# Output projection of a Mamba2 layer with tokens on the output partitions, one matmul group moved ahead of another, and one unused state dropped

## The reference, cut to what matters

```
x = x + 0.5 * ffn(layernorm(x))
x = x + mamba2(layernorm(x))       # 64 heads of 64 channels, state size 128, conv of 4 taps
x = x + 0.5 * ffn(layernorm(x))

# the end of mamba2, per token:
hidden = (Y_diag + Y_off + D * xs) * silu(gate)          # 4096 channels
var    = mean(hidden * hidden)
hidden = hidden * rsqrt(var + EPS) * norm_w
return hidden @ out_proj_w                               # 4096 -> 256

# the state that one chunk hands to the next:
state[c + 1] = chunk_decay[c] * state[c] + states[c]
```

## Time and profile before

| | us |
|---|---|
| median of 3 runs | 1360.67 (1360.49 to 1361.19) |
| the profiled execution | 1359.91 |
| its span, first to last instruction | 1358.2 |
| TensorE busy with matmuls | 1299.9 (96%) |
| VectorE busy | 1187.0 (87%) |
| ScalarE busy | 1001.7 (74%) |
| GpSimd busy | 851.0 (63%) |

### The profile page before, as it was taken

One profiled execution on the slowest core, in us unless ns is written; L12 is line 12 of the kernel. 1 busy time (PEld: TensorE's weight loads), 2 busy tenths in 40 slices (PEclk: granted clock), 3 DMA queues, 4 the chain that ended last, 5 costly groups with the idle time before them and its releaser, 6 DMA issues.

```text
span 1358.2 us, 26981 instructions
## 1 busy us (share of the span) xinstructions
PE 1299.9 (96%) x8896; PEld 1111.2 (82%) x8896; DVE 1187.0 (87%) x2651; ACT 1001.7 (74%) x2043; POOL 851.0 (63%) x920
## 2 busy tenths in 40 slices
PE   7999998899999999999999999999999999987998
PEld 7988886678888888888888888888888888876887
DVE  6965567899999999999999999999999999997542
ACT  1135566898888888889888888888898888883432
POOL 1033220268697878778787978787787879674232
PEclk9999999999999999999999999999999999998999
DMA  7110002265555543544555555436446544345000
GB/s 163 80 69 32 17 16 70 71 137 125 108 126 116 119 119 109 115 106 110 120 124 107 123 118 123 112 110 113 106 115 120 123 115 115 100 103 202 16 17 32
DMA packets 98106, 136.51 MB, mean 101 GB/s; under 512 B 23760, under 2 KB 45872, under 8 KB 97840
## 3 DMA queue, kind: packets, MB, share of 16 engines
q1 hardware_dynamic: 97968, 134.78, 41.7%
HBM read 124.78 MB, written 9.96 MB: 99 GB/s over the span
## 4 chain that ended last, share of the span: by engine, by line
PE 56%; DVE 29%; issue 11%; ACT 3%; DMA 0%; DVEq 0%; POOL 0%; SPq 0%; ACTq 0%; POOLq 0%
PE psum L38 13%; PE psum L40 12%; PE psum L39 12%; DVE xs L1266 6%; PE psum L1715 6%; DVE inner L1317 4%; PE psum L1704 4%; PE psum L1495 4%; DVE M L1293 3%; PE psum L1692 3%; DVE xend L1283 3%; DVE psum L1325 3%; DVE mixed L1347 2%; PE psum L1681 1%; DVE carry L1317 1%
## 5 line engine op out<-in xcount | busy, mean ns | idle before, releaser
L826 ACT ACTIVATE M<-cum_row,cum_table 128x128 f32<-128x128 f32 x1024 | 312.1, 390 | 0.0
L1266 DVE SCALAR_TENSOR_TENSOR xs<-psum,conv_w_sb,xs 128x509 f32<-128x509 f32 (+2 forms) x384 | 283.1, 737 | 0.4
L986 POOL TENSOR_TENSOR hid_lo<-hid,hid_hi 128x512 fp32r<-128x512 f32 x128 | 204.9, 1601 | 56.1 <-PE psum L40 49.9
L1032 POOL TENSOR_TENSOR hid<-hid,sg 128x512 f32<-128x512 f32 x128 | 165.8, 1295 | 76.4 <-DVE hid L1334 76.2
L1018 POOL TENSOR_TENSOR squares<-squares,sq 128x512 f32<-128x512 f32 x124 | 161.1, 1299 | 71.8 <-ACT sq L803 71.8
L1293 DVE TENSOR_TENSOR M<-M,CB 128x1024 f32<-128x1024 f32 x128 | 184.4, 1440 | 0.0
L1715 PE MATMUL psum<-M,xdt 128*64 128x128 f32 x2048 | 140.1, 278 | 20.2 <-DVE psum L1325 20.0
L1715 PEld LDWEIGHTS psum<-M,xdt 128*64 128x64 f32 x2048 | 110.1, 136 | 42.8 <-DVE M L1293 24.2
L1692 PE MATMUL psum<-xend,B_tok 128*128 128x128 f32 x1024 | 137.6, 277 | 5.3 <-DVE carry L1317 4.5
L840 ACT ACTIVATE xs<-psum,conv_b_sb,conv_w_sb 128x512 f32<-128x512 f32 x128 | 99.2, 775 | 57.3 <-PE psum L40 56.6
L834 ACT ACTIVATE M<-M 128x1024 f32<-128x1024 f32 x128 | 134.5, 1051 | 0.5
(11 more groups left out here) (197 smaller groups left out, 3379.1 us busy)
## 6 DMA issues: line engine op xcount, KB each, us to landing
cum_row<-cum_scratch SPq DMA_DIRECT2D x256, 256.0 KB, 4.6
e_row<-e_scratch SPq DMA_DIRECT2D x256, 128.0 KB, 3.5
xw_raw<-L_attn_in_proj_w_dram SPq DMA_DIRECT2D x32, 128.0 KB, 5.0
wo_raw<-L_attn_out_proj_w_dram SPq DMA_DIRECT2D x32, 128.0 KB, 4.5
gw_raw<-L_attn_in_proj_w_dram SPq DMA_DIRECT2D x16, 256.0 KB, 5.5
x_res<-_attn_hidden_states_dram SPq DMA_DIRECT2D x4, 512.0 KB, 7.1
x_scratch<-x_res SPq DMA_DIRECT2D x4, 512.0 KB, 2.6
x_res<-x_scratch SPq DMA_DIRECT2D x1, 2048.0 KB, 8.5
```

The costliest lines, as they stand in the source:

```text
L826: last = nc.scalar.activation(M[:, v % 3, h, c * CH:(c + 1) * CH], cum_row[:, v % 2, h, c * CH:(c + 1) * CH], ACT.Relu, bias=scalar_of(CUM ...
L986: nc.gpsimd.tensor_tensor(hid_lo[:], hid[:, v % 2, :], hid_hi[:, v % 2, :].bitcast(F32), ALU.subtract).then_inc(hid_lo_done, 1)
L1032: nc.gpsimd.tensor_tensor(hid[:, v % 2, :], hid[:, v % 2, :], sg[:, v % 8, :], ALU.mult).then_inc(hid_done, 1)
L1266: nc.vector.scalar_tensor_tensor(xs[:, v % 7, shift:], psum[:, X_BANK + v % 2, 0:TT - shift], tap_of(v, step), xs[:, v % 7, shift:], ALU.m ...
```

## The change

Four things are done. (1) `out_proj` holds 128 tokens of the hidden values in the array and streams the 256 columns of the output weights, for each of the slot's 4 chunks: 12 matmuls of 256 columns in place of 6 of 512. `mixed` then has tokens on the partitions, and `turn_mixed` goes, with its semaphore. `second_residual` reads `mixed` from SBUF. (2) TensorE does proj_g(s+8) ahead of diag(s+1). (3) VectorE does skip_path(s+1) behind tap 2 and scan 2. (4) The last chunk's state isn't made any more: on the last tile `to_chunk_end` and `states` work on 3 chunks, not 4.

```diff
-    mixed = sb("mixed", [P, KT, L], F32)
+    mixed = sb("mixed", [P, NC, D], F32)
...
-                nc.vector.tensor_tensor(xend[:], psum[:, XT_BANK, :].rearrange("p (c h q) -> p c h q", h=2, q=HP),
-                                        per_chunk_head(TO_END, v), ALU.mult).then_inc(xend_done, 1)
+                n = min(CPT, NC - 1 - at_slot(v)[1] * CPT)
+                nc.vector.tensor_tensor(xend[:, 0:n], psum[:, XT_BANK, 0:n * P].rearrange("p (c h q) -> p c h q", h=2, q=HP),
+                                        per_chunk_head(TO_END, v)[:, 0:n], ALU.mult).then_inc(xend_done, 1)
...
                 for m in range(KT):
+                    rows = mixed[:, t * CPT + 2 * m:t * CPT + 2 * m + 2, :].rearrange("p s d -> p (s d)")
                     if v < SLOTS:
-                        nc.vector.tensor_copy(mixed[:, m, tile(t)], psum[:, OUT_BANK + m, :]).then_inc(mixed_done, 1)
+                        nc.vector.tensor_copy(rows, bank(OUT_BANK + m)).then_inc(mixed_done, 1)
                     else:
-                        nc.vector.tensor_tensor(mixed[:, m, tile(t)], psum[:, OUT_BANK + m, :], mixed[:, m, tile(t)],
-                                                ALU.add).then_inc(mixed_done, 1)
+                        nc.vector.tensor_tensor(rows, bank(OUT_BANK + m), rows, ALU.add).then_inc(mixed_done, 1)
...
-                dve.wait_ge(mixed_turned, T + 1)
+                dve.wait_ge(mixed_done, KT * (ALL // GP - NT + T + 1))
                 for s in range(T * CPT, (T + 1) * CPT):
-                    half = psum[:, mixed_banks(T)[s % CPT // 2], s % 2 * D:(s % 2 + 1) * D]
-                    nc.vector.scalar_tensor_tensor(x3[:, s, :], half, rms[:, s:s + 1], x3[:, s, :],
+                    nc.vector.scalar_tensor_tensor(x3[:, s, :], mixed[:, s, :], rms[:, s:s + 1], x3[:, s, :],
                                                    ALU.mult, ALU.add).then_inc(x2_done, 1)
...
-                if alive(s + 1):
-                    skip_path(s + 1)
                 if alive(s + 7):
                     conv_tap(s + 7, 2)
                 if alive(s + 2):
                     scan(s + 2, 2)
+                if alive(s + 1):
+                    skip_path(s + 1)
...
-                for c in range(CPT):
+                for c in range(min(CPT, NC - 1 - t * CPT)):
                     last = nc.tensor.matmul(psum[:, ST_BANK, c * P:(c + 1) * P], B_tok[:, t * CPT + c, :],
...
-                for m in range(KT):
-                    cols = slice(m * P, (m + 1) * P)
-                    last = split_matmul(nc, psum[:, OUT_BANK + m, :], wo_hi[:, j, cols], wo_lo[:, j, cols],
-                                        hid_hi[:, v % 2, :], hid_lo[:], start=(j == 0), stop=(j == GP - 1))
+                for c in range(CPT):
+                    toks = slice(c * CH, (c + 1) * CH)
+                    last = split_matmul(nc, bank(OUT_BANK + c // 2)[:, (c % 2) * D:(c % 2 + 1) * D],
+                                        hid_hi[:, v % 2, toks], hid_lo[:, toks], wo_hi[:, j, :], wo_lo[:, j, :],
+                                        start=(j == 0 and c % 2 == 0), stop=(j == GP - 1), skip=True)
...
+                if alive(s + 8):
+                    proj_g(s + 8)
                 if alive(s + 1):
                     diag(s + 1)
...
                 if alive(s + 8):
-                    proj_g(s + 8)
                     proj_x(s + 8)
...
-                if s == ALL - 3:
-                    turn_mixed(0)
...
-                if k % MT == 0 and T < NT:
-                    turn_mixed(T)
                 if k % MT == 3 and T < NT:
+                    pe.wait_ge(mixed_done, KT * (ALL // GP))
+                    if T > 1:
+                        pe.wait_ge(ln3.lo_done, KT * T)
                     ln3.tensor_turn(pe, T)
```

More of the change, by code:

```diff
@@ L396, in macaron @@
     sums_psum, rms_var, rms_sd_ready, rms_step = sem("sums_psum"), sem("rms_var"), sem("rms_sd_ready"), sem("rms_step")
-    mixed_turned, x2_done = sem("mixed_turned"), sem("x2_done")
+    x2_done = sem("x2_done")
     halo_in, halo_step, halo_done = sem("halo_in"), sem("halo_step"), sem("halo_done")
@@ L458, in turn_banks @@
         return (2, 3) if T == 0 else (6, 7)
-    def mixed_banks(T):
-        return (0, 1) if T == 0 else (6, 7)
     def alive(v):
@@ L1743, in sum_squares @@
                 last.then_inc(sums_psum, 1)
-            def turn_mixed(T):
-                if T == 0:
-                    pe.wait_ge(conv_done, ALL)
-                    pe.wait_ge(mixed_done, KT * (ALL // GP - NT + 1))
-                else:
-                    pe.wait_ge(mixed_done, KT * (ALL // GP))
-                    if T > 1:
-                        pe.wait_ge(ln3.lo_done, KT * T)
-                for s in range(T * CPT, (T + 1) * CPT):
-                    for m in range(KT):
-                        at = s % 2 * D + m * P
-                        last = nc.tensor.transpose(psum[:, mixed_banks(T)[s % CPT // 2], at:at + P],
-                                                   mixed[:, m, s * CH:(s + 1) * CH], ident[:])
-                last.then_inc(mixed_turned, 1)
             pe.wait_ge(const_done, 5)
```

## The result

The change makes the kernel faster by 1.0%, as forecast. The median goes from 1360.58 (1360.09 to 1361.19, 4 runs) to 1347.14 us (1344.1 to 1348.61, 4 runs), the ratio is 0.9898 [0.9881, 0.9916]. (Ratios are taken over all the runs, with a 95% interval, and can differ from the quotient of the two medians by up to 0.0008.) The forecast was 1346 and its own range 1340 to 1352. The profiled execution has a span of 1345.5 us, where the one before had 1358.2, so 12.7 us have to be found between the two traces.

The account below looks back on a forecast made before the run. TensorE and VectorE were taken to bound the loop by turns. From 1359.91 us: -11.9 seven groups, -0.8 ramp, -2.7 transposes, -0.5 last slots, +1.5 residual gives 1345.5 profiled, median 1346; own range 1340 to 1352, 8 in 10 1334 to 1360.

Parts of the forecast that it names:

- What bounds: Steady loop: TensorE and VectorE stop each other by turns; sums 120.9 and 122.1 of a 124.2 us group.
- Output projection: TensorE's 12 matmuls of 256 columns for 6 of 512: 0.045 us more a slot, 0.7 a group.
- Rival (d): Loop's output projection: weight loads add 0.1 us a matmul, 1.2 a slot, over 140 in all; chance 0.03.
- Last state: A group's last tile: 0.22 us a chunk, 0.9 a group off TensorE; narrower `to_chunk_end` takes 0.6 off VectorE.
- Order: Loop, proj_g ahead of `diag`: its 16.7 us of waits go; `states` may wait next, up to 5 us.
- Rival (c): Loop: `diag`'s waits only move to `states`; a group loses 0.4 us, kernel 1356; chance 0.14.
- The matched pair: Loop: `diag` ends 1.4 us later, skip path moves back 1.04; nearly matched, VectorE may wait 0 to 0.1.
- GpSimd and the mask: VectorE's mask: five slots wait 0.33 us more for `hid_hi`, two 0.4 less; +0.8 a group, mean 1.45 to 1.55.
- The ramp and the last slots: Loop's two ends: half a group of ramp gives 0.8 us; last four slots lose a chunk's state, giving 0.5.
- The end: Behind the loop: dropping `turn_mixed` of tiles 1 to 3 gains 2.7 us; tile 0's `second_residual` costs 1.5 (0 to 4.2).
- (a): Loop: complete decoupling, masks find GpSimd free more often; group falls to TensorE's 120.7 us, kernel 1333; chance 0.16.
- (b): Mask's start: moved skip path makes it wait for GpSimd; decides from 0.17 us more a slot; kernel 1366; chance 0.15.

Follow-up runs that it names:

- order alone: Kernel before with only the two moves (proj_g ahead of diag, skip path behind scan 2); old output projection, all states kept: 1346.17 us, 0.9901.
- the two attempts: Changed kernel with GpSimd's `hid_hi` waiting until the mask is done, 1356.5 us (0.9982); changed kernel with `hid_hi` made by ScalarE, 1403.49 us (1.0324).

## Why the prediction was right, point by point

**What bounds.** It said that two engines stop each other in turns, and that an edit is worth what it does to both sums. Shown: the moves, which remove no work, gave nearly all of the time (order alone 0.9901). What it did not say is that VectorE would then hold the loop nearly alone. Its sum was put at 122.3 and is 121.75, 0.5 under the group. The added work of the projection came to half its size in time, 0.39 of 0.8 a group, and so did the saved state, 0.42 on top of the order for 0.9 of TensorE and 0.6 of VectorE.

**Output projection.** +0.045 a slot was forecast and 0.051 measured. Rival (d), 0.1 a matmul, did not come. The price read from a layer with the same shapes held. The prediction's other price, by TensorE: Matmul & The Clock Gate, section Back-to-back issue gap, of the Trainium skill, used a formula that this page gives for an isolated matmul and not for a stream; no sum rests on it.

**Last state.** 0.22 a chunk was right, and `to_chunk_end` takes 0.54 with three chunks for 0.67 with four, 0.13 less where 0.14 was put. Together they take 0.7 off a group by themselves.

**Order.** `diag`'s waits for `scale_off` were to go and did, 16.7 to none. `states` was to be next, in the slots of `add_out`, with up to 5 us; it waited 5.1, but behind one `add_out` in four. VectorE's waits for `diag` ahead of the skip path do not appear in the answer for 330 to 1190 us. Rival (c), in which the waits only move, did not come. The matched pair was shown by the two kernels with one move each, 125.98 and 123.42 a group for 122.25.

**GpSimd and the mask.** This is the step whose size came out and whose account did not. Five slots in a group were to wait shortly for `hid_hi`, and two were to have a long wait shortened. The mean came to 1.467, inside 1.45 to 1.55: +0.4 a group over all slots, +0.6 over slots 8 to 119, where +0.8 was put. But no mask waited for `hid_hi`; those that waited met the gate product. And the moves by themselves left the mean where it was (1.436); it rose to 1.467 only where the last state was dropped as well, with the old projection (1.467) as with the new. Why dropping a state shifts the masks that way was not tried. That the measured group, 122.25, is so near 122.5 is therefore partly luck. What the forecast didn't see is that GpSimd waits in the same way. VectorE's row of the changed kernel, then GpSimd's:

```profile
704.28 1.80 DVE L1291 TENSOR_TENSOR M<-M,CB 128x1024 f32<-128x1024 f32 x1
```

```profile
703.71 1.30 POOL L1029 TENSOR_TENSOR hid<-hid,sg 128x512 f32<-128x512 f32 x1
705.07 1.49 POOL L980 CAST hid_hi<-hid 128x512 fp32r<-128x512 f32 x1
```

The mask met the gate, which ended at 705.01, and took 1.80. The cast then met the mask, which ended at 706.08, and took 1.49 where it has 0.62 alone. Its mean is 1524 ns. No cost of it shows here: GpSimd is busy for 66% and has 0% of the chain that ended last. With the order alone it has 16% of that chain.

**The ramp and the last slots.** Half a group of ramp was to give 0.8, and the stretch to slot 8's mask lost 0.5. That can't be judged, since the same loop took 1.8 more in another execution. The last slots gave 1.9 where 0.5 was put. The term left out the moves: the order alone gives 2.7 there (42.29 for 44.97). From step 120 on TensorE has no projections of x and gate left; why the moves are worth that much in these slots was not tried.

**The end** is the term that was mis-sized. Forecast: -2.7 for the transposes and +1.5 for the port, together -1.2. Measured: +3.0 up to the last layer's first matmul and -0.8 behind it, together +2.2. Of the +3.0, 2.1 are the two products that met GpSimd (2.99 for 0.88); the other 0.9 is a small product of the statistics (L1368), which took 1.15 beside GpSimd where it had taken 0.28. That one isn't the projection's: with the old projection and the new order it took 1.21. It is GpSimd's squares of the slot before. They ran from 1218.12 to 1219.40, that is 0.76 behind the start of the last skip path, where in the trace before they began 0.11 ahead of it (1232.12 for 1232.23). The product began 0.9 behind the skip path in both and in both it ended with them. The stated bounds, 0 to 4.2, held it. Behind the first matmul, tiles 2 and 3 gave 0.9 each as forecast, and tile 1, which was to give 0.9 too, lost 1.0. TensorE's row there, first of the kernel before, then of the changed one:

```profile
1260.27 1.41 PE L193 MATMUL psum<-ident,xn 128*128 128x128 f32 x8 [0.17 <-DVE xn L184]
```

```profile
1249.57 1.32 PE L193 MATMUL psum<-ident,xn 128*128 128x128 f32 x8 [1.68 <-DVE xn L184]
```

TensorE came to the transposes of the norm earlier and waited 1.68 for VectorE where it had waited 0.17. The 0.8 of `turn_mixed` had been cover for VectorE's norm. And the norm itself starts 1.1 later, counted from the last layer's first matmul (15.2 for 14.1). Half of that is there at VectorE's first product of the layer (5.30 for 4.75), where more of the stretch at half clock lies behind that matmul; then a product of tile 1's residual took 1.27, not 0.47, beside GpSimd, and the missing wait for the transposes gave 0.3 back. "A stretch where TensorE has no wait" was true of the trace before, but by 0.17 only, and the edit itself shifts VectorE by the port. The kernel before also had a stretch of 10.2 us at half clock there, the changed one of 13.7 us, of which 3.5 against 4.7 us lie behind the last layer's first matmul (rows further down).

**The sum.** The loop gave 1.7 more than forecast and the end 3.4 less, so a good part of the small error (12.7 us found, 14.4 forecast between the profiled executions) is two misses against each other.

**Rivals.** (a) was out, since a group stopped at 122.25, 1.45 above TensorE's sum. (b), the mask paying for the late skip path, decided from 0.17 more a slot and had 0.03 (0.04 over slots 8 to 119); by its own terms 0.2 more makes 1363 us, not 1364. Not tried was a kernel in which a mask never meets GpSimd, so TensorE's sum as the floor below VectorE's is argued and not shown; the two attempts brought other waits in.

## What to carry to other kernels

Where two engines each wait for the other by turns, reorder first: moving one block on each engine by the same amount gave 1.0%; of the two moves alone one was worth some 0.5 us a group, the other made the kernel slower. Price a change of form by rows of the same shape elsewhere in the kernel; that held to 0.006 us a slot. Then ask at the seams what the removed work had covered (here 0.8 us of transposes hid a norm), which engine's idle time is left (here 0.5 us a group of VectorE, so that saving TensorE's work brings half), and whether a new source puts a VectorE instruction with two SBUF inputs beside a busy GpSimd: the version that left the output projection as it was is 0.3% faster still.

## What the runs showed of the hardware

- Two products of 256 columns with both inputs in SBUF took 2.99 us beside GpSimd and 0.88 with one input in PSUM. A product of 12 columns took 0.28 or 1.15 at the same place of the program. The price is what is left of GpSimd's instruction, not the size of VectorE's.
- The start times of a trace don't say by themselves which of the two gives way. In 33 slots the cast of GpSimd is shown starting up to 0.1 us ahead of the mask, and the mask took 1.2 and the cast 1.7 to 1.8, against 0.61 alone.
- On TensorE a change to `diag`'s matmuls from those of the full array costs about 0.1 us wherever `diag` stands (128*64 in its rows). The start of its block is 0.20 us behind the start of the last transpose, where two transposes are 0.11 apart; with `proj_g` ahead of it is 0.33, where two of these are 0.23 apart. So the new order was neutral for TensorE: transposes, `proj_g`, `diag` and `proj_x` make 4.45 us in either.
- The granted clock falls to half, 0.50, for 10 to 14 us at the seam of these two kernels, where TensorE waits for the last layer's input and is busy for 7.3 of 10.2 and 8.8 of 13.7 us; in most of the profiled executions (9 of 13) also near 200 us, and in some near 1190 us. In the changed kernel this last stretch begins at 1186.5, right after 3.4 us in which TensorE was busy for 1.1. The rows are stretches: window, length, busy time of TensorE, its weight loads, VectorE, ScalarE and GpSimd, granted clock, DMA share, GB/s. Before, then changed:

```profile
195.00:210.00 15.00, 12.97 (x79) 11.76 (x78) 8.54 (x24) 7.31 (x11) 1.79 (x2) 0.89 0.16 53
...
1238.20:1248.40 10.20, 7.29 (x25) 5.99 (x24) 5.47 (x20) 3.26 (x6) 0.00 (x0) 0.50 0.12 50
```

```profile
1186.50:1189.90 3.40, 3.40 (x18) 3.07 (x20) 2.81 (x8) 3.37 (x6) 2.94 (x3) 0.50 0.42 102
...
1224.00:1237.70 13.70, 8.78 (x31) 7.39 (x30) 7.81 (x26) 3.26 (x6) 0.10 (x1) 0.50 0.11 44
```

With the order alone, the first of these stretches was granted 1.00:

```profile
195.00:210.00 15.00, 11.84 (x81) 10.23 (x80) 9.52 (x32) 8.79 (x14) 2.58 (x2) 1.00 0.24 72
```

and its first mask started at 242.48, where that of the changed kernel started at 245.06. In the four traces without that stretch the first mask starts at 242.4 to 243.1, in the nine with it at 244.5 to 246.1. Between the order alone and the changed kernel 1.1 of the 2.6 us are there before 70 us, so the stretch makes about 1.5. They are no effect of an edit in the loop. The kernel before and the changed one both had this stretch, but only the changed one had that at 1186.5; what makes a stretch come was not tried.
